# Mixer tiles of a Mamba-2 block: D product moved to the tile's end, x transposed in halves, y's halves added after the masked decays

## The chip, the cores and the metric

One core of a Trainium2 chip runs the whole program. The metric is the device time of one execution in microseconds (us). Of the kernel before there are three timed executions and one more that was profiled. The engines are named as in the profile: PE is TensorE (PEld its weight loads), DVE is VectorE, ACT is ScalarE, POOL is GpSimd, SP is SyncE.

## The reference, cut to what matters

2048 tokens of width 512 (two sequences of 1024) go through an expert feed-forward block, a Mamba-2 mixer and a second feed-forward block. The change touches the mixer alone:

```python
zxbcdt = layernorm(x) @ W_in.T              # z, x, B, C, dt
x, B, C = silu(causal_conv4(xBC) + conv_b)  # x: 16 heads of 64
dt = softplus(dt + dt_bias); dA = exp(-exp(A_log) * dt)
state = dA * state + x[..., None] * (dt * B)     # step by step along the sequence
y = C . state + D * x
yg = y * silu(z)
out = (yg * rsqrt(mean(yg * yg) + eps) * norm_w) @ W_out.T   # added to the residual
```

## The kernel before

The recurrence is worked in tiles of 128 tokens. A sequence is one turn `i` of a loop and has two groups `j` of four tiles `q`, so there are 2 x 2 x 4 = 16 tiles; `n` counts the eight tiles of a turn. Each group begins with nine weight units (projection, convolution, decay sums, the gate z), and then come the four tiles, the subject of the change. In one tile:

- **decays** (PE, `decays(n, q, g)`, L1925 and L1929): for each quarter `g` of the heads the exponent of the masked decay goes into one of two banks; ACT takes the exponential into L (L1006). The next quarter in the same bank waits for that.
- **G** (PE, L1945, L1946): C x B and B transposed; ACT copies both to GB (L1013).
- **x in rows** (PE, L1950): eight transposes into banks 4 and 5. DVE makes xdt = x dt (L1473) and xD = x D (L1485) of them; POOL makes xw from xdt (L722).
- **M**: DVE multiplies L by C x B in place, a quarter at a time (L1497). These instructions read two tiles of SBUF.
- **C x S** (PE, L1966): C times the carried state, into banks 6 and 7; DVE multiplies it by its decays into y, "yc" below (L1508), and POOL adds xD to y (L729).
- **D product** (PE, L1980): B x xw into banks 4 and 5, which DVE adds to the state that POOL has decayed (L717, L1522, L1523).
- **M x xdt** (PE, L1988): 16 matmuls (32 records), one for each head, into banks 6 and 7. DVE adds each half to y (L1529) and POOL multiplies it by silu(z) (L734).
- **The next step for the tile before**: y_features (PE, L1818) transposes the gated y in two halves into banks 6 and 7, ACT writes its high part (`y_hi`) and DVE its low part (`y_lo`, L1057), and project (PE, L1834) multiplies it by W_out. ACT sums the squares (L958), POOL makes the root of their mean (`rms`, L698 to L700), and DVE adds the result to the residual (L1374). For the first tile of a group (q = 0) there is no tile before in its stream: that one's features and projection stand among the next group's first units, or at the end of the turn.
- **The next group's input**: DVE takes statistics of one tile (L1043 to L1049), POOL their root (L614, L615), DVE scales it (L1054), PE transposes it (L1973), ACT and DVE split it (L756, L1057).

The order on each engine is written out by hand and each engine works its own list in order. Semaphores tie the lists: `after(s, n, ...)` waits until `s` has been raised n times in this turn. PE's order in a tile is decays 0 and 1, G, x in rows, decays 2, y_features(n-1), decays 3, project(n-1), C x S, the transposes of the next input, D product, M x xdt. DVE's is statistics, xdt, y_lo(n-1), xD, scale, M 0 to 3, residual(n-1), yc, xb low part, the two state additions, the two additions to y.

Of the kernel before, what the change touches and what calls it, by code (L numbers as in the profile page):

```python
# [8 lines left out]
P = 128  # L9
# [100 lines left out]
def program(nc, x, w_router, w_gate, w_up, w_down, w_in, w_dt, conv, heads, norm_w, w_out, out):  # L110
# [356 lines left out]
    with block:  # L467
# [118 lines left out]
        def _(pool):  # L586
# [84 lines left out]
            def mixer(k):  # L671
# [12 lines left out]
                def turn(i):  # L684
# [17 lines left out]
                    for j in range(BPB):  # L702
# [5 lines left out]
                        for q in range(TB):  # L708
                            n = j * TB + q
                            hq = slice(q * HEADS, (q + 1) * HEADS)  # L710
                            pool.wait_ge(l_var, i * TPB + (n + TB + 1))
                            rsqrt_ln(slice(q, q + 1), l_rstd)
# [6 lines left out]
                                               each(dec[:, hq], HD), ALU.mult).then_inc(m_Sd, 1)  # L719
                            after(m_xdt, n + 1, TPB)  # L720
# [4 lines left out]
                            if q >= 1:  # L725
                                rms(n - 1)
# [23 lines left out]
        def _(act):  # L750
# [157 lines left out]
            def mixer(k):  # L908
# [10 lines left out]
                def turn(i):  # L919
# [40 lines left out]
                    for j in range(BPB):  # L960
# [39 lines left out]
                        for q in range(TB):  # L1000
                            n = j * TB + q
                            for g in range(HG):
                                after(m_B, HG * n + g + 1, HG * TPB)
                                after(m_E, 2 * n, 2 * TPB)
                                for h in range(g * GH, (g + 1) * GH):
                                    ins = act.activation(L[:, h], bank[g % 2][:, (h % GH) * P:(h % GH + 1) * P], ACT.Exp,  # L1006
                                                         bias=ncs[:, q * HEADS + h:q * HEADS + h + 1])
                                ins.then_inc(m_L, 1)
                                if g == 0:
                                    after(m_G, n + 1, TPB)  # L1010
                                    after(m_D, n, TPB)
                                    after(m_M, HG * n, HG * TPB)
                                    act.activation(GB[:], bank[3][:, 0:2 * P], ACT.Copy).then_inc(m_Bt, 1)  # L1013
                                if g == 1 and q >= 1:
                                    y_hi(n - 1)
                            if q >= 1:
                                squares(n - 1)

# [18 lines left out]
        def _(dve):  # L1037
# [314 lines left out]
            def mixer(k):  # L1352
                nf, nm = phase_counts(k)
                wait_residual(dve, k)
                def turn(i):
# [21 lines left out]
                    for j in range(BPB):  # L1377
# [78 lines left out]
                        for q in range(TB):  # L1456
# [8 lines left out]
                            ln_stats([x_next], [q], l_var)  # L1465

                            for half in range(2):
                                hs = slice(half * DI // 2, (half + 1) * DI // 2)
                                after(m_xt, 2 * n + half + 1, 2 * TPB)
                                if half == 0:  # L1470
                                    after(m_xw, n, TPB)
                                    after(m_E, 2 * n, 2 * TPB)
                                ins = dve.tensor_tensor(heads_of(xdt[:, hs]), heads_of(bank[4 + half][:]),  # L1473
                                                        each(dts[:, q * HEADS + half * HB:q * HEADS + (half + 1) * HB], HD),
                                                        ALU.mult)
                                if half == 0:
                                    own.mark(ins)
                            ins.then_inc(m_xdt, 1)
                            if q >= 1:
                                y_lo(n - 1)  # L1480

                            after(m_yd, n, TPB)
                            for half in range(2):
                                hs = slice(half * DI // 2, (half + 1) * DI // 2)
                                ins = dve.tensor_tensor(heads_of(xD[:, hs]), heads_of(bank[4 + half][:]),  # L1485
                                                        each(hp[:, 2 * HEADS + half * HB:2 * HEADS + (half + 1) * HB], HD),
                                                        ALU.mult)
                                if half == 0:
                                    own.mark(ins)
                            ins.then_inc(m_xD, 1)  # L1490
# [4 lines left out]
                            for g in range(HG):  # L1495
                                after(m_L, HG * n + g + 1, HG * TPB)
                                dve.tensor_tensor(L[:, g * GH:(g + 1) * GH], L[:, g * GH:(g + 1) * GH],  # L1497
                                                  some(GB[:, 0:P], GH), ALU.mult).then_inc(m_M, 1)
                            if q >= 1:
                                residual(n - 1)  # L1500

# [4 lines left out]
                            for half in range(2):  # L1506
                                hs = slice(half * DI // 2, (half + 1) * DI // 2)
                                ins = dve.tensor_tensor(heads_of(y[:, n % 2, hs]), heads_of(bank[6 + half][:]),  # L1508
                                                        each(ecs[:, q * HEADS + half * HB:q * HEADS + (half + 1) * HB], HD),
                                                        ALU.mult)  # L1510
                                if half == 0:
                                    own.mark(ins)
                            ins.then_inc(m_yc, 1)
# [3 lines left out]
                                    xb[:, 0, :, q * P:(q + 1) * P], l_lo)  # L1517

# [5 lines left out]

                            after(m_yd, n + 1, TPB)
                            for half in range(2):
# [528 lines left out]
```

## Time and profile before

| what | value |
|---|---|
| median of 3 executions | 1613.78 us (1613.63 to 1614.77) |
| profiled execution, its own time | 1616.87 us |
| its span, first to last instruction | 1615.1 us |
| PE busy | 1522.0 us (94%) |
| DVE busy | 1044.0 us (65%) |
| ACT busy | 750.3 us (46%) |
| POOL busy | 796.0 us (49%) |
| mean granted TensorE clock | 0.976 |

Starts and durations in the trace are counted from the start of the span of 1615.1 us. The profiled execution took 3.1 us more than the median. A granted clock of 1.00 is the engine's 2.4 GHz and 0.50 is 1.2 GHz.

### The profile page before, as it was taken

To read this page: it belongs to the slowest core of one execution; us is meant where nothing else is said; L and a number is where in the kernel's file an instruction comes from. 1 tells how busy PE (TensorE), PEld (TensorE's weight loads), DVE (VectorE), ACT (ScalarE), POOL (GpSimd) and SP (SyncE) were. 2 spreads that over 40 slices of the span, in tenths; PEclk is the share of its full clock that TensorE was granted. 3 is DMA by queue.
4 is the path that set the end of the run, shared out by engine and by line. 5 is a ranking of instruction groups with operands and counts; after the bars stand their busy time and mean duration, and the time that the engine had idled before them with its cause. 6 is when DMAs were issued, how large, how long until landed. Compare 5 with 4: busy or idle time off the path is not lost. (4 is left out here: it accounts for less than half of the span.)

```text
span 1615.1 us, 23935 instructions
## 1 busy us (share of the span) xinstructions
PE 1522.0 (94%) x8530; PEld 1294.3 (80%) x8530; DVE 1044.0 (65%) x1739; ACT 750.3 (46%) x1290; POOL 796.0 (49%) x491
## 2 busy tenths in 40 slices
PE   6989999999999989999988999999889999999999
PEld 6767999989877777787767778778668999999877
DVE  7664565666467877677657767766564666666465
ACT  4211666666512654454445345434222666666411
POOL 2101777776444435535534553553021777666442
PEclk9999999999999999999999999998999999999999
DMA  7032687867443120020012001014222787777243
GB/s 291 27 108 62 215 284 254 283 244 255 173 166 99 53 79 1 17 76 27 1 50 70 1 27 66 1 37 162 69 68 93 249 276 257 270 272 266 75 161 127
DMA packets 70873, 214.42 MB, mean 133 GB/s; under 512 B 8097, under 2 KB 8097, under 8 KB 69857
## 3 DMA queue, kind: packets, MB, share of 16 engines
q1 hardware_dynamic: 48672, 155.18, 27.2%
q0 software_dynamic: 11360, 37.23, 7.8%
q10 hardware_dynamic: 10720, 20.45, 3.5%
q8 instruction: 70, 1.15, 0.3%
q14 instruction: 51, 0.41, 0.1%
HBM read 179.80 MB, written 33.03 MB: 132 GB/s over the span
## 5 line engine op out<-in xcount | busy, mean ns | idle before, releaser
L626 POOL TENSOR_TENSOR g_lo<-g_raw,g_hi 128x1408 fp32r<-128x1408 f32 x54 | 179.4, 3322 | 259.4 <-ACT g_hi L756 258.9
L626 POOL TENSOR_TENSOR u_lo<-u_raw,u_hi 128x1408 fp32r<-128x1408 f32 x54 | 174.5, 3231 | 67.9 <-ACT u_hi L756 67.9
L1674 PE MATMUL bank<-u_hi,xgT 128*128 128x352 f32 x624 | 168.5, 333 | 0.0
L1674 PE MATMUL bank<-g_hi,xgT 128*128 128x352 f32 x624 | 162.7, 323 | 0.0
L1697 PE MATMUL bank<-d_hi,hT 128*128 128x512 f32 (+1 forms) x468 | 159.8, 395 | 1.8 <-DVE hT L1057 1.8
L691 POOL TENSOR_TENSOR w_hl<-w_raw,w_hl 128x1024 fp32r<-128x1024 f32 x36 | 88.8, 2468 | 144.7 <-ACT w_hl L756 144.7
L1626 PE MATMUL bank<-xs,g_hi 128*128 128x512 f32 (+1 forms) x384 | 129.8, 421 | 7.5 <-DVE gate L1203 6.6
L1642 PE MATMUL bank<-d_hi,hT 128*128 128x512 f32 (+1 forms) x384 | 126.1, 401 | 5.9 <-DVE hT L1057 3.5
L804 ACT ACTIVATE gate<-bank 128x512 f32<-128x512 f32 (+1 forms) x48 | 28.6, 596 | 220.5 <-PE bank L1626 212.8
L1057 DVE TENSOR_TENSOR hT<-bank,hT 128x384 fp32r<-128x384 f32 x78 | 43.0, 552 | 128.9 <-ACT hT L756 128.9
L1388 DVE SCALAR_TENSOR_TENSOR acc<-pre,cw,acc 128x512 f32<-128x512 f32 x120 | 121.8, 1015 | 4.3
L1212 DVE TENSOR_TENSOR d_lo<-d_raw,d_hi 128x1024 fp32r<-128x1024 f32 x54 | 106.3, 1968 | 27.2 <-ACT d_hi L756 19.5
L1874 PE MATMUL bank<-xs,w_hl 128*128 128x512 f32 x480 | 115.2, 397 | 7.2 <-issue 5.0
L1626 PE MATMUL bank<-xs,u_hi 128*128 128x512 f32 (+1 forms) x384 | 120.8, 396 | 0.0
L668 POOL DMA_INDIRECT yg<-routed_y,slots x64 | 67.6, 1057 | 97.4 <-DVE X L1235 56.6
L1911 PE MATMUL bank<-w_hl,xs 128*128 128x256 f32 x768 | 101.1, 295 | 14.3 <-ACT zs L989 10.9
L1674 PEld LDWEIGHTS bank<-g_hi,xgT 128*128 128x128 f32 x624 | 111.0, 188 | 3.6
L1874 PEld LDWEIGHTS bank<-xs,w_hl 128*128 128x128 f32 x480 | 90.7, 191 | 28.2 <-issue 8.9
L1911 PEld LDWEIGHTS bank<-w_hl,xs 128*128 128x128 f32 x768 | 98.7, 203 | 16.8 <-ACT zs L989 11.7
L1674 PEld LDWEIGHTS bank<-u_hi,xgT 128*128 128x128 f32 x624 | 110.5, 188 | 0.0
L1057 DVE TENSOR_TENSOR d_lo<-d_raw,d_hi 96x512 fp32r<-96x512 f32 x54 | 109.4, 2025 | 0.0
L1697 PEld LDWEIGHTS bank<-d_hi,hT 128*128 128x128 f32 (+1 forms) x468 | 87.9, 188 | 21.2 <-DVE hT L1057 4.7
(254 smaller groups left out, 3676.8 us busy)
## 6 DMA issues: line engine op xcount, KB each, us to landing
g_raw<-in_w_gate SPq DMA_DIRECT2D x54, 704.0 KB, 5.8
u_raw<-in_w_up SPq DMA_DIRECT2D x54, 704.0 KB, 7.0
d_raw<-in_w_down SPq DMA_DIRECT2D x54, 512.0 KB, 5.3
w_raw<-in_w_in SPq DMA_DIRECT2D x37, 512.0 KB
routed_y<-ys ACTq DMA_DIRECT2D x32, 512.0 KB
d_raw<-in_w_down SPq DMA_DIRECT2D x54, 192.0 KB, 5.6
token_x<-xn SPq DMA_DIRECT2D x8, 1024.0 KB, 5.2
X<-in_x SPq DMA_DIRECT2D x4, 1024.0 KB, 10.1
```

What stands on the lines that cost most here:

```text
L626: pool.tensor_tensor(half_of(piece, 1, s), raw_at[piece][s % RING][:], half_of(piece, 0, s).bitcast(F), ALU.subtract)\
L668: pool.indirect_dma_start(yg[:, t % 2, slot], None, routed_y, slot_rows(slot * NT + t))\
L691: pool.tensor_tensor(w_hl[:, w % 2, 1], w_raw[:, w % 2], w_hl[:, w % 2, 0].bitcast(F), ALU.subtract).then_inc(m_wlo, 1)
L1057: dve.tensor_tensor(hl_lo, value, hl_hi.bitcast(F), ALU.subtract).then_inc(signal, 1)
L1212: dve.tensor_tensor(lo[:, 0:2], raw[:, 0:2], hi[:, 0:2].bitcast(F), ALU.subtract)
L1388: ins = dve.scalar_tensor_tensor(acc[:, c % 2], pre[:, c % 2, tap:tap + D], cw[:, c, tap:tap + 1], acc[:, c % 2], ALU.mult, ALU.add)
L1626: ins = pe.matmul(dst[0:fw, 0:width], half_of(part, hw, s)[:, kc, f0:f0 + fw], x_of(hx, kc), start=(n == 0), stop=(n == 3 * KD - 1))
L1642: ins = pe.matmul(bank[4 + a][:], hT[0:fw, hh, c, a * P:(a + 1) * P], half_of(2, hw, s)[0:fw, c], start=(c == 0 and m == 0), stop=(c == NF ...
L1674: ins = pe.matmul(dst[:, 0:FE], xgT[:, n % 2, hx, kc], half_of(piece, hw, NS + j)[:, kc], start=(m == 0), stop=(m == 3 * KD - 1))
L1697: ins = pe.matmul(bank[Y + n % 2][:], hT[0:fw, hh, c, 0:P], half_of(2, hw, NS + j)[0:fw, c], start=(m == 0), stop=(m == 3 * NF - 1))
L1874: ins = pe.matmul(bank[c % 2][:], wt[:, hw, kc, (c % 2) * P:(c % 2 + 1) * P], xb[:, hx, kc], start=(m == 0), stop=(m == 3 * KD - 1))
L1911: ins = pe.matmul(bank[6 + half][:, (q % 2) * WU:(q % 2 + 1) * WU], xb[:, hx, kc, q * P:(q + 1) * P], wt[:, hw, kc], start=(m == 0), stop= ...
```

## The change

On PE, the two halves of y_features(n-1) stand before decays 0 and after decays 1. The x transposes are split: the first half before G, the second after decays 2. C x S follows; then come decays 3 and project(n-1). M x xdt comes ahead of the D product, which is the last work of the tile. On ACT, `y_hi` of each half stands before the exponentials of quarters 0 and 1; the squares and the copy to GB stand before quarter 2. On DVE, y_lo(n-1) comes first, xdt waits for both halves of x, and then come scale, M 0, xD, yc, M 1 to 3, the low part of xb, the first addition to y, residual(n-1), the second addition to y and the state additions. On POOL, the decay of S comes before the layer-norm root, and rms(n-1) comes before xw. No operation is added or left out. The diff, with the common indentation and blank lines taken off:

```diff
--- before.py
+++ after.py
@@ -708,8 +708,6 @@
 for q in range(TB):
     n = j * TB + q
     hq = slice(q * HEADS, (q + 1) * HEADS)
-    pool.wait_ge(l_var, i * TPB + (n + TB + 1))
-    rsqrt_ln(slice(q, q + 1), l_rstd)
     after(m_dec, j + 1, BPB)
     after(m_C, n, TPB)
     after(m_S, n, TPB)
@@ -717,13 +715,15 @@
     pool.tensor_tensor(S[:, (n + 1) % 2].rearrange("p (h d) -> p h d", d=HD),
                        S[:, n % 2].rearrange("p (h d) -> p h d", d=HD),
                        each(dec[:, hq], HD), ALU.mult).then_inc(m_Sd, 1)
+    pool.wait_ge(l_var, i * TPB + (n + TB + 1))
+    rsqrt_ln(slice(q, q + 1), l_rstd)
+    if q >= 1:
+        rms(n - 1)
     after(m_xdt, n + 1, TPB)
     after(m_D, n, TPB)
     pool.tensor_tensor(xw[:].rearrange("p (h d) -> p h d", d=HD),
                        xdt[:].rearrange("p (h d) -> p h d", d=HD),
                        each(wd[:, hq], HD), ALU.mult).then_inc(m_xw, 1)
-    if q >= 1:
-        rms(n - 1)
     after(m_yc, n + 1, TPB)
     after(m_xD, n + 1, TPB)
     pool.tensor_tensor(y[:, n % 2], y[:, n % 2], xD[:], ALU.add).then_inc(m_yd, 1)
@@ -1000,22 +1000,21 @@
 for q in range(TB):
     n = j * TB + q
     for g in range(HG):
+        if g < 2 and q >= 1:
+            y_hi(n - 1, (g,))
+        if g == 2:
+            if q >= 1:
+                squares(n - 1)
+            after(m_G, n + 1, TPB)
+            after(m_D, n, TPB)
+            after(m_M, HG * n, HG * TPB)
+            act.activation(GB[:], bank[3][:, 0:2 * P], ACT.Copy).then_inc(m_Bt, 1)
         after(m_B, HG * n + g + 1, HG * TPB)
         after(m_E, 2 * n, 2 * TPB)
         for h in range(g * GH, (g + 1) * GH):
             ins = act.activation(L[:, h], bank[g % 2][:, (h % GH) * P:(h % GH + 1) * P], ACT.Exp,
                                  bias=ncs[:, q * HEADS + h:q * HEADS + h + 1])
         ins.then_inc(m_L, 1)
-        if g == 0:
-            after(m_G, n + 1, TPB)
-            after(m_D, n, TPB)
-            after(m_M, HG * n, HG * TPB)
-            act.activation(GB[:], bank[3][:, 0:2 * P], ACT.Copy).then_inc(m_Bt, 1)
-        if g == 1 and q >= 1:
-            y_hi(n - 1)
-    if q >= 1:
-        squares(n - 1)
     act.wait_ge(l_tp, i * TPB + (n + TB + 1))
     split_hi(xb[:, 0, :, q * P:(q + 1) * P], bank[3][:].rearrange("p (c t) -> p c t", c=KD), l_hi)
 y_hi(TPB - 1)
@@ -1462,72 +1461,69 @@
         nxt = dve.snap(nxt % NT)
     x_next = X[:, bass.ds(nxt, 1), :].rearrange("p o n -> p (o n)")
-    ln_stats([x_next], [q], l_var)
-    for half in range(2):
+    def halves(tile, coefs, width, signal):
+        for half in range(2):
+            hs = slice(half * DI // 2, (half + 1) * DI // 2)
+            ins = dve.tensor_tensor(heads_of(tile[:, hs]), heads_of(bank[width + half][:]),
+                                    each(coefs[half], HD), ALU.mult)
+            if half == 0:
+                own.mark(ins)
+        ins.then_inc(signal, 1)
+    of_heads = lambda t, at: [t[:, at + half * HB:at + (half + 1) * HB] for half in range(2)]
+    def decayed(g):
+        after(m_L, HG * n + g + 1, HG * TPB)
+        dve.tensor_tensor(L[:, g * GH:(g + 1) * GH], L[:, g * GH:(g + 1) * GH],
+                          some(GB[:, 0:P], GH), ALU.mult).then_inc(m_M, 1)
+    def y_add(half):
         hs = slice(half * DI // 2, (half + 1) * DI // 2)
-        after(m_xt, 2 * n + half + 1, 2 * TPB)
-        if half == 0:
-            after(m_xw, n, TPB)
-            after(m_E, 2 * n, 2 * TPB)
-        ins = dve.tensor_tensor(heads_of(xdt[:, hs]), heads_of(bank[4 + half][:]),
-                                each(dts[:, q * HEADS + half * HB:q * HEADS + (half + 1) * HB], HD),
-                                ALU.mult)
-        if half == 0:
-            own.mark(ins)
-    ins.then_inc(m_xdt, 1)
+        after(m_E, 2 * n + half + 1, 2 * TPB)
+        dve.tensor_tensor(y[:, n % 2, hs], y[:, n % 2, hs], bank[6 + half][:], ALU.add)\
+            .then_inc(m_yi, 1)
     if q >= 1:
         y_lo(n - 1)
-    after(m_yd, n, TPB)
-    for half in range(2):
-        hs = slice(half * DI // 2, (half + 1) * DI // 2)
-        ins = dve.tensor_tensor(heads_of(xD[:, hs]), heads_of(bank[4 + half][:]),
-                                each(hp[:, 2 * HEADS + half * HB:2 * HEADS + (half + 1) * HB], HD),
-                                ALU.mult)
-        if half == 0:
-            own.mark(ins)
-    ins.then_inc(m_xD, 1)
+    ln_stats([x_next], [q], l_var)
+    after(m_xt, 2 * n + 2, 2 * TPB)
+    after(m_xw, n, TPB)
+    after(m_E, 2 * n, 2 * TPB)
+    halves(xdt, of_heads(dts, q * HEADS), 4, m_xdt)
     dve.wait_ge(l_rstd, i * TPB + (n + TB + 1))
     dve.wait_ge(l_tp, i * TPB + (n + TB - 1))
     ln_scale(xn_m[:, q % 2], x_next, q).then_inc(l_xn, 1)
     after(m_Bt, n + 1, TPB)
-    for g in range(HG):
-        after(m_L, HG * n + g + 1, HG * TPB)
-        dve.tensor_tensor(L[:, g * GH:(g + 1) * GH], L[:, g * GH:(g + 1) * GH],
-                          some(GB[:, 0:P], GH), ALU.mult).then_inc(m_M, 1)
-    if q >= 1:
-        residual(n - 1)
+    decayed(0)
+    after(m_yd, n, TPB)
+    halves(xD, of_heads(hp, 2 * HEADS), 4, m_xD)
     after(m_C, n + 1, TPB)
     after(m_dec, j + 1, BPB)
     after(m_F, 2 * (n - 1), 2 * TPB)
     after(m_sq, n - 1, TPB)
-    for half in range(2):
-        hs = slice(half * DI // 2, (half + 1) * DI // 2)
-        ins = dve.tensor_tensor(heads_of(y[:, n % 2, hs]), heads_of(bank[6 + half][:]),
-                                each(ecs[:, q * HEADS + half * HB:q * HEADS + (half + 1) * HB], HD),
-                                ALU.mult)
-        if half == 0:
-            own.mark(ins)
-    ins.then_inc(m_yc, 1)
+    halves(y[:, n % 2], of_heads(ecs, q * HEADS), 6, m_yc)
+    decayed(1)
+    decayed(2)
+    decayed(3)
     dve.wait_ge(l_hi, i * TPB + (n + TB + 1))
     lo_half(xb[:, 1, :, q * P:(q + 1) * P], bank[3][:].rearrange("p (c t) -> p c t", c=KD),
             xb[:, 0, :, q * P:(q + 1) * P], l_lo)
+    after(m_yd, n + 1, TPB)
+    y_add(0)
+    if q >= 1:
+        residual(n - 1)
+    y_add(1)
     after(m_D, n + 1, TPB)
     after(m_Sd, n + 1, TPB)
     new = S[:, (n + 1) % 2]
     own.mark(dve.tensor_tensor(new[:, 0:DI // 2], new[:, 0:DI // 2], bank[4][:], ALU.add))
     dve.tensor_tensor(new[:, DI // 2:DI], new[:, DI // 2:DI], bank[5][:], ALU.add).then_inc(m_S, 1)
-    after(m_yd, n + 1, TPB)
-    for half in range(2):
-        hs = slice(half * DI // 2, (half + 1) * DI // 2)
-        after(m_E, 2 * n + half + 1, 2 * TPB)
-        dve.tensor_tensor(y[:, n % 2, hs], y[:, n % 2, hs], bank[6 + half][:], ALU.add)\
-            .then_inc(m_yi, 1)
 y_lo(TPB - 1)
 residual(TPB - 1)
 settle((m_xw, TPB), (m_yd, TPB), (m_E, 2 * TPB), (m_F, 2 * TPB), (m_sq, TPB), (m_out, TPB),
@@ -1934,28 +1930,31 @@
 for q in range(TB):
     n = j * TB + q
     tt = slice(q * P, (q + 1) * P)
+    def x_rows(half):
+        for c in range(4):
+            ins = pe.transpose(bank[4 + half][:, c * P:(c + 1) * P],
+                               xc[:, 2 + 4 * half + c, tt], ident[:])
+        ins.then_inc(m_xt, 1)
+    if q >= 1:
+        y_features(n - 1, (0,))
     decays(n, q, 0)
     decays(n, q, 1)
+    if q >= 1:
+        y_features(n - 1, (1,))
     if q == 0:
         after(m_xc, (j + 1) * NCH, BPB * NCH)
+    after(m_S, n, TPB)
+    x_rows(0)
     after(m_Bt, n, TPB)
     after(m_dtc, j + 1, BPB)
     pe.wait_ge(l_lo, i * TPB + (n + TB))
     pe.matmul(bank[3][:, 0:P], xc[:, 0, tt], xc[:, 1, tt], start=True, stop=True)
     pe.transpose(bank[3][:, P:2 * P], xc[:, 0, tt], ident[:]).then_inc(m_G, 1)
-    after(m_S, n, TPB)
-    for half in range(2):
-        for c in range(4):
-            ins = pe.transpose(bank[4 + half][:, c * P:(c + 1) * P],
-                               xc[:, 2 + 4 * half + c, tt], ident[:])
-        ins.then_inc(m_xt, 1)
     decays(n, q, 2)
-    if q >= 1:
-        y_features(n - 1)
-    decays(n, q, 3)
-    if q >= 1:
-        project(n - 1)
+    x_rows(1)
     pe.wait_ge(m_zero, i + 1)
     after(m_yi, 2 * n, 2 * TPB)
@@ -1966,6 +1965,9 @@
         ins = pe.matmul(bank[6 + half][:], xc[:, 1, tt], S[:, n % 2, half * 512:(half + 1) * 512],
                         start=True, stop=True)
     ins.then_inc(m_C, 1)
+    decays(n, q, 3)
+    if q >= 1:
+        project(n - 1)
     pe.wait_ge(l_xn, i * TPB + (n + TB + 1))
     after(m_Bt, n + 1, TPB)
@@ -1974,14 +1976,7 @@
                            ident[:])
     ins.then_inc(l_tp, 1)
-    after(m_xw, n + 1, TPB)
-    after(m_xD, n + 1, TPB)
-    for half in range(2):
-        ins = pe.matmul(bank[4 + half][:], Bt, xw[:, half * 512:(half + 1) * 512],
-                        start=True, stop=True)
-    ins.then_inc(m_D, 1)
     after(m_yc, n + 1, TPB)
     for g in range(HG):
         after(m_M, HG * n + g + 1, HG * TPB)
         for h in range(g * GH, (g + 1) * GH):
@@ -1989,6 +1984,13 @@
                             xdt[:, h * HD:(h + 1) * HD], start=True, stop=True)
         if g % 2:
             ins.then_inc(m_E, 1)
+    after(m_xw, n + 1, TPB)
+    after(m_xD, n + 1, TPB)
+    for half in range(2):
+        ins = pe.matmul(bank[4 + half][:], Bt, xw[:, half * 512:(half + 1) * 512],
+                        start=True, stop=True)
+    ins.then_inc(m_D, 1)
 y_features(TPB - 1)
 project(TPB - 1)
```

## Rows read from the trace of the kernel before

**Rows 1.** Waits of PE, 537 to 1092 us: who waited for whom, us in total, times, longest.
```profile
PE bank L1834 <- DVE yT L1057: 7.5, 12, 0.6
```
**Rows 2.** Timeline, a later tile (q = 2): start us, us, engine, line, operation, count.
```profile
633.12 0.38 PE L1925 MATMUL bank<-mask_b,ident_b 128*128 128x512 bf16 x1
...
635.70 1.04 PE L1818 MATMUL bank<-ident,y 128*128 128x128 f32 x8
...
636.34 1.09 ACT L756 ACTIVATE yT<-bank 128x512 fp32r<-128x512 f32 x2
...
636.97 1.29 DVE L1057 TENSOR_TENSOR yT<-bank,yT 128x512 fp32r<-128x512 f32 x2 [0.56 <-ACT yT L756]
...
637.81 5.69 PE L1834 MATMUL bank<-wo,yT 128*128 128x512 f32 x24 [0.63 <-DVE yT L1057]
...
643.33 1.88 PE L1966 MATMUL bank<-S,xc 128*128 128x512 f32 x4
...
645.49 1.88 PE L1980 MATMUL bank<-xw,GB 128*128 128x512 f32 x4
...
647.20 3.68 PE L1988 MATMUL bank<-xdt,L 128*128 128x64 f32 x32
...
649.21 0.69 DVE L1529 TENSOR_TENSOR y<-y,bank 128x512 f32<-128x512 f32 x1 [0.52 <-PE bank L1988]
649.97 1.27 POOL L734 TENSOR_TENSOR y<-y,zs 128x512 f32<-128x512 f32 x1 [1.00 <-DVE y L1529]
...
650.72 0.38 PE L1925 MATMUL bank<-mask_b,ident_b 128*128 128x512 bf16 x1
```
**Rows 3.** Timeline, the same tile: what DVE and POOL do.
```profile
633.92 0.69 DVE L1043 BATCH_NORM_STATS2 stats<-X 128x6 f32 x1
...
635.12 1.29 DVE L1473 TENSOR_TENSOR xdt<-bank,dts 128x512 f32<-128x512 f32 x2
...
638.18 1.28 DVE L1485 TENSOR_TENSOR xD<-bank,hp 128x512 f32<-128x512 f32 x2
...
640.07 2.49 DVE L1497 TENSOR_TENSOR L<-L,GB 128x512 f32<-128x512 f32 x4
...
646.62 2.36 POOL L729 TENSOR_TENSOR y<-y,xD 128x1024 f32<-128x1024 f32 x1 [4.26 <-DVE y L1508]
```
**Rows 4.** Timeline, a group's first tile (q = 0).
```profile
600.93 0.39 PE L1925 MATMUL bank<-mask_b,ident_b 128*128 128x512 bf16 x1
...
602.85 1.29 DVE L1473 TENSOR_TENSOR xdt<-bank,dts 128x512 f32<-128x512 f32 x2 [1.76 <-PE bank L1950]
...
603.40 1.15 ACT L1006 ACTIVATE L<-bank,ncs 128x128 f32<-128x128 f32 x4
...
604.60 0.39 PE L1925 MATMUL bank<-mask_b,ident_b 128*128 128x512 bf16 x1 [1.36 <-ACT L L1006]
...
605.53 2.08 POOL L722 TENSOR_TENSOR xw<-xdt,wd 128x1024 f32<-128x1024 f32 x1
605.78 2.38 DVE L1497 TENSOR_TENSOR L<-L,GB 128x512 f32<-128x512 f32 x1
...
606.36 3.63 PE L1966 MATMUL bank<-S,xc 128*128 128x512 f32 x4
...
611.99 3.68 PE L1988 MATMUL bank<-xdt,L 128*128 128x64 f32 x32
```
**Rows 5.** Windows, the same tile: us, busy of PE, PEld, DVE, ACT, POOL, clock, DMA.
```profile
607.00:608.00 1.00, 1.00 (x2) 0.34 (x1) 1.00 (x1) 0.92 (x4) 0.61 (x1) 0.50 0.00 0
```
**Rows 6.** Timeline, a group's units: the convolution's three taps, undisturbed, then with POOL.
```profile
679.26 2.33 DVE L1388 SCALAR_TENSOR_TENSOR acc<-pre,cw,acc 128x512 f32<-128x512 f32 x3
...
681.70 4.35 DVE L1388 SCALAR_TENSOR_TENSOR acc<-pre,cw,acc 128x512 f32<-128x512 f32 x3
...
681.97 2.75 POOL L691 TENSOR_TENSOR w_hl<-w_raw,w_hl 128x1024 fp32r<-128x1024 f32 x1
```
**Rows 7.** Timeline, PE at the end of the first turn.
```profile
798.48 3.68 PE L1988 MATMUL bank<-xdt,L 128*128 128x64 f32 x32
...
804.99 7.04 PE L1834 MATMUL bank<-wo,yT 128*128 128x512 f32 x24
```

## The prediction

> **What bounds the kernel now.** I read the page first, for the shares: PE is busy nearly throughout, so time is won only where PE waits. Then I read PE's waits over the mixer. The one wait that each later tile (q = 1 to 3) repeats is the projection's for the low part of the transposed y: 12 times, 7.5 us in all [rows 1]. The timeline of one such tile shows why: transposes at 635.70, ACT's high part at 636.34, DVE's low part at 636.97, projection at 637.81, after a wait of 0.63. The tile lasts 650.72 - 633.12 = 17.60 us [rows 2]. From rows of PE I take strides (start to start): projection 643.33 - 637.81 = 5.52, M x xdt with the step to the next tile 3.52 (3.42 without), D product 647.20 - 645.49 = 1.71 and C x S the same; eight transposes 0.88, a quarter's decays 0.44, G 0.38, the input's four transposes 0.44 [rows 2].
>
> The first tile of a group is another matter: there the time goes by DVE. From 600.93 on, xdt starts after 1.92 us. The first masked decay then takes 2.38 us, where four take 2.49 in a later tile [rows 3, 4]. It stood at 605.78 and ended 0.55 after POOL's xw ended at 607.61: while POOL works, a DVE instruction that reads two tiles of SBUF stands still. After three more of about 0.6, the decays end at 609.97, as does C x S at 609.99, though that ran at clock 0.50 (1.2 GHz) [rows 4, 5]: the low clock cost next to nothing there. M x xdt starts at 611.99, 11.06 us into the tile. With 3.52 the tile is 14.58.
>
> **The change, later tiles.** Let s be the start of the first half of y_features.
> - The previous M x xdt began at s - 5.2 (3.42, D product 1.71, a step of 0.07). DVE adds y's first half 2.01 after its start and POOL's gating ends 4.04 after it [rows 2], so the first transposes don't wait. The second half's gating ends near 5.75, s + 0.55, and its transposes come at s + 1.32.
> - ACT follows by 0.64: y_hi 0 at s + 0.64, exponentials (1.15) from s + 1.13, y_hi 1 at s + 2.2. DVE's low part follows by 0.63, at s + 2.83, and PE by 0.84 after that: C x S at s + 3.67. PE's own work ahead of it is 3 x 0.44 of decays, 0.88 of y, 0.88 of x and 0.38 of G, 3.46. What is left of the wait is 0.2, now before C x S.
> - Then C x S 1.71, decays 0.44, projection 5.52 and transposes 0.44: M x xdt at s + 11.78, the next tile at s + 17.0. I take **0.6 gained** on each of 12 tiles, 7.2 us. Both ends: nothing gained, or 0.8 with no wait at all.
> - The cover on DVE: low part to s + 3.5, statistics 1.2, xdt 1.25, scale 0.7 at most (between xD's end and M [rows 3]), M 0 0.6, xD and yc 2.5: yc ends at s + 9.7. M 1 to 10.3; POOL's addition of xD (2.36) goes next and holds M 2 back until 12.7, ended at 13.3, M 3 at 13.9. PE needs M 2 at 11.78 + 1.71 = 13.5 and M 3 at 14.35. It holds, by 0.2 us. With this cover gone, each microsecond of delay is one of the tile.
> - xw is behind rms on POOL, and so behind M 0 on DVE, by some 0.4 us. The D product needs xw only at s + 15.2. POOL's root of the statistics is now behind the decay of S, done by s + 3.4, before the statistics exist. No DMA is moved, and SP has no part in a tile.
>
> **The first tiles.** Here nothing hides the new order. Quarter 2's decays wait for ACT's first exponentials: 603.40 + 1.15, PE at 604.60, which is 3.67 [rows 4]. Half of x now stands behind them, at 4.11. DVE's xdt needs both halves and starts 0.64 later, at 4.75 instead of 1.92, and ends at 6.04. POOL's xw begins at 6.1 and goes ahead of M 0, as before, since scale stands between xdt and M 0: xw ends at 8.2, M 0 at 8.8. xD and yc (2.4) end at 11.2. M x xdt starts at 11.35, only 0.3 later than before. But M 1 to 3 are now behind yc: M 1 ends at 11.8, POOL adds xD until 14.05, M 2 ends at 14.6, M 3 at 15.2. PE does two quarters by 13.1, waits, starts quarter 2 at 14.75, has both by 16.5, and then the D product: 18.2 instead of 14.58, **3.6 lost**.
>
> That POOL gets in between M 1 and M 2 is the disputed price. The nearest row: taps at 681.70 took 4.35 instead of 2.33, and POOL's instruction 2.75 [rows 6], so POOL waited for one tap and then held up the other two. Those taps are parted by waits, M 1 to 3 are not. If POOL comes last instead, y waits for it and the next tile starts at about 17.4: 2.8 lost. I take the first value, as the row is of the same two engines.
>
> The Trainium skill ("SBUF — State Buffer", Who interferes with whom) says that VectorE with two SBUF inputs and a GpSimd instruction that reads SBUF exclude each other, and "Issue order, not op shape, decides who blocks". It speaks against this change, which puts M 1 to 3 right beside POOL's addition, where before they stood ahead of it. The trace agrees, with the 2.38 of the first M [rows 4]. By the page alone M 1, issued first, holds POOL, and then POOL holds M 2, which is the same 3.6.
>
> **The clock** fell to 0.50 in such a tile before [rows 5], after PE had waited for ACT, and for about 3.5 us, as C x S took 3.63 instead of 1.88 [rows 2, 4]. In the new order PE waits about 2.4 us before M x xdt and 1.65 between quarters. A second fall would now meet work on the path: 3.5 us at half speed add up to 1.7. I take 0.3, since much of it would fall into waits. So a first tile costs 3.9, bounded by 1.2 (the faster rival, below) and 3.6 + 1.7 = 5.3; four cost **15.6**.
>
> **End of a turn** (two). Before, from M x xdt to the projection 804.99 - 798.48 = 6.51 [rows 7], with the D product 1.71 ahead: 8.22. Now 5.2, then transposes with a wait of 0.15, ACT 0.64 after their start, the low part behind the state additions at 6.6, projection at 7.4. Gained 0.8 each, **1.7**. The 24 matmuls took 7.04 there instead of 5.69; if the clock stays up, 1.35 more each. Groups that end without a turn gain nothing of their own.
>
> **Sum**: 15.6 - 7.2 - 1.7 = +6.7. The profiled execution, at 1616.87, would go to 1623.6. It stands 3.1 above the median, so the median goes to 1613.78 + 6.7, about **1620**, 0.4% slower. About 0.2% (3.2 us) is what a measurement of this kernel can tell from no change.
>
> **The rivals.**
> - *Forecast (0.58)*: later tiles gain, first tiles lose more. With its bounds 1616 (2.8 lost in each first tile: 11.2 - 8.9 = +2.3) to 1631 (5.3 lost, and 0.2 gained in a later tile: 21.2 - 2.4 - 1.7 = +17.1).
> - *Faster (0.18)*: VectorE isn't held up in the first tiles. If M 0 goes ahead of xw, yc ends at 9.5; if M 1 to 3 go ahead of POOL's addition, M x xdt runs through from 9.65 and y's chain ends the tile near 15.8. Lost 1.2: 4.8 - 7.2 - 1.7 = -4.1, 1609.7. For it: in later tiles rms's small instructions did not slow the four M. Against: the 2.38. It decides when a first tile loses less than 1.4 us.
> - *About the same (0.18)*: only one of the two goes VectorE's way, 2.3 lost: 9.2 - 8.9 = +0.3, 1614. A weaker form: gain and loss are each a third off.
> - *Much slower (0.06)*: in later tiles xw starts ahead of M 0 and takes 1.9 us off a cover of 0.2. A tile becomes 1.2 longer than before: 15.6 + 14.4 - 1.7 = +28, 1642. Against it: rms stands before xw.
>
> **Range.** 1610 to 1631 takes in the forecast with its bounds and the same-time case, and the edge of the faster one; it leaves out most of the faster and the much slower case. Faster 0.18, same 0.20, slower 0.62.
>
> **What would show it.** Later tiles: period near 17.0, no wait before the projection, 0.2 before C x S. First tiles: xdt about 4.75 after the first decays, an M of over 2 us beside xw and another beside POOL's addition, PE waiting for M between quarters 1 and 2 of M x xdt, tile near 18.2. Turn end: projection 0.8 earlier. The prediction is wrong if first tiles stay under 16 us, or later ones stay at 17.6.

## The result, and the profile of the kernel after

The median went from 1613.7 us (1612.38 to 1614.77, four runs) to **1635.88 us** (1633.47 to 1637.94, four runs): a ratio of 1.0137, with a 95% interval of [1.0117, 1.0157]. Slower was the likeliest sign of the prediction. Its 1620 is 16 us too low, though, and the time lies outside its range of 1610 to 1631. The profiled execution took 1637.94 us with a span of 1636.2, so the spans differ by 21.1.

The page first. PE is busy for 12.7 us more (1522.0 before) with the same 8530 instructions, and four more slices show a clock under 0.9: its matmuls have become slower. DVE is busy for 27.9 us more (1044.0 before) with the same 1739 instructions: its masked decays, which now stand still beside POOL, take 82.8 us instead of 46.6, and its other instructions 8.3 less.

```profile
span 1636.2 us, 23919 instructions
...
PE 1534.7 (94%) x8530; PEld 1302.9 (80%) x8530; DVE 1071.9 (66%) x1739; ACT 749.4 (46%) x1290; POOL 798.7 (49%) x491
...
PEclk9999999999999998998999899898999999999999
```

The waits of PE over the mixer (537 to 1112 us) of the kernel after, answering to [rows 1]; the columns are the total in us, the number and the longest:

```profile
PE bank L1983 <- DVE y L1468: 14.5, 4, 4.0
...
PE bank L1921 <- ACT L L1015: 7.4, 4, 1.8
...
PE bank L1830 <- DVE yT L1056: 2.1, 2, 1.1
...
PE bank L1983 <- DVE L L1479: 1.3, 2, 0.8
```

The projection's twelve waits (7.5 us) are gone; the two that are left are the turn ends. In their place stand four waits of M x xdt for yc, one in each group's first tile, 14.5 us in all. The wait for M 2, on which the prediction spent most of its words, is 1.3 us in two tiles.

A later tile (q = 1 of the first group) of the kernel after, rows of PE, DVE and POOL from its timeline, answering to [rows 2, 3]; the columns are start and duration in us, engine, line, operation and count:

```profile
624.86 0.60 PE L1814 MATMUL bank<-ident,y 128*128 128x128 f32 x4
...
627.65 0.69 DVE L1056 TENSOR_TENSOR yT<-bank,yT 128x512 fp32r<-128x512 f32 x1 [0.70 <-ACT yT L756]
...
628.49 1.96 PE L1965 MATMUL bank<-S,xc 128*128 128x512 f32 x4
...
631.11 0.69 DVE L1479 TENSOR_TENSOR L<-L,GB 128x512 f32<-128x512 f32 x1
...
631.57 1.99 POOL L724 TENSOR_TENSOR xw<-xdt,wd 128x1024 f32<-128x1024 f32 x1
...
634.10 4.08 DVE L1479 TENSOR_TENSOR L<-L,GB 128x512 f32<-128x512 f32 x3
...
636.71 3.68 PE L1983 MATMUL bank<-xdt,L 128*128 128x64 f32 x32
...
642.00 0.60 PE L1814 MATMUL bank<-ident,y 128*128 128x128 f32 x4
```

With s = 624.86 the low part comes at s + 2.79, C x S at s + 3.63, M x xdt at s + 11.85 and the next tile at s + 17.14. The prediction had 2.83, 3.67, 11.78 and 17.0. The addition of xD does get between the three M (4.08 instead of 1.9), but PE never waits for them.

The first tile of the second group of the kernel after, answering to [rows 4]:

```profile
742.51 0.39 PE L1921 MATMUL bank<-mask_b,ident_b 128*128 128x512 bf16 x1
...
747.27 1.29 DVE L1468 TENSOR_TENSOR xdt<-bank,dts 128x512 f32<-128x512 f32 x2 [4.58 <-PE bank L1936]
...
748.64 2.13 POOL L724 TENSOR_TENSOR xw<-xdt,wd 128x1024 f32<-128x1024 f32 x1 [0.78 <-DVE xdt L1468]
...
748.93 2.39 DVE L1479 TENSOR_TENSOR L<-L,GB 128x512 f32<-128x512 f32 x1
...
753.64 4.04 DVE L1479 TENSOR_TENSOR L<-L,GB 128x512 f32<-128x512 f32 x3
753.77 7.04 PE L1983 MATMUL bank<-xdt,L 128*128 128x64 f32 x32 [3.93 <-DVE y L1468]
753.80 2.73 POOL L729 TENSOR_TENSOR y<-y,xD 128x1024 f32<-128x1024 f32 x1 [3.02 <-DVE y L1468]
...
760.61 3.73 PE L1991 MATMUL bank<-xw,GB 128*128 128x512 f32 x4
...
764.12 0.73 PE L1814 MATMUL bank<-ident,y 128*128 128x128 f32 x4
```

And the granted clock there, from the windows of the same kernel (stretch; clock in the third column from the right). A window's mean tells how much of it was at 0.50: 0.57 means 0.86 us of it, 0.81 means 0.38.

```profile
753.00:754.00 1.00, 0.23 (x2) 0.23 (x3) 1.00 (x3) 0.00 (x0) 0.20 (x1) 1.00 0.00 0
754.00:755.00 1.00, 1.00 (x7) 1.00 (x7) 1.00 (x2) 0.00 (x0) 1.00 (x1) 0.57 0.00 0
...
758.00:759.00 1.00, 1.00 (x7) 1.00 (x6) 0.88 (x2) 0.00 (x0) 0.04 (x1) 0.50 0.00 0
764.00:765.00 1.00, 1.00 (x8) 0.74 (x7) 0.63 (x2) 0.11 (x1) 0.00 (x0) 0.81 0.00 0
```

Up to M x xdt the tile goes as worked out: xdt at 4.76, M x xdt at 11.26. Then the clock falls to 0.50 (1.2 GHz) at 754.14, 0.37 us into M x xdt and right behind PE's wait of 3.93, and comes back at 764.38, 10.2 us later, after the D product. M x xdt took 7.04 instead of 3.68, the D product 3.73 instead of 1.94. The same 10.2 us stand in all four first tiles (in the first group the fall comes inside the wait, at 614.19), where the kernel before had one stretch of 3.4 under C x S [rows 5]. Up to the next tile's transposes a tile lasts 21.6 to 21.7 us. In the last two groups the low clock reaches into the next tile; counted from the first decays to the next M x xdt, less the 11.85 of an undisturbed tile, the four are 21.7 to 22.1, 21.9 in the mean, against 14.57 before.

**The books.** Four first tiles: 4 x 7.3 = 29.2 lost. Twelve later ones, at 17.11 to 17.14 instead of 17.60: 6.0 gained. Two turn ends: 4.1 gained (below). Together +19.1 of the 21.1. The rest stands ahead of the first group, whose first decays come at 603.19 instead of 600.93, 2.3 later; the trace after has one low-clock stretch more there (563 to 566). The change does not touch that part; in the profiled executions of the twelve experiments the same decays come anywhere from 596.87 (9) to 602.68 (11), so it is spread between executions.

### The profile page after: what moved, and what is told of

The parts are those of the page before. It is cut to its first block and busy times, and to the rows that moved or that the text cites. A ratio compares the mean times of both kernels' runs of the same rounds, so it can differ in the third digit from the quotient of the medians.

```text
span 1636.2 us, 23919 instructions
## 1 busy us (share of the span) xinstructions
PE 1534.7 (94%) x8530; PEld 1302.9 (80%) x8530; DVE 1071.9 (66%) x1739; ACT 749.4 (46%) x1290; POOL 798.7 (49%) x491
## 3 DMA queue, kind: packets, MB, share of 16 engines
q8 instruction: 70, 1.15, 0.3%
## 5 line engine op out<-in xcount | busy, mean ns | idle before, releaser
L1907 PEld LDWEIGHTS bank<-w_hl,xs 128*128 128x128 f32 x768 | 98.5, 203 | 16.3 <-ACT zs L989 11.7
```

What stands on the lines that cost most here:

```text
L1907: ins = pe.matmul(bank[6 + half][:, (q % 2) * WU:(q % 2 + 1) * WU], xb[:, hx, kc, q * P:(q + 1) * P], wt[:, hw, kc], start=(m == 0), stop= ...
```

## The experiments

Three things had to be told apart: whether the first tiles alone lose, what in them costs the clock, and what the POOL additions beside the masked decays cost. The first four kernels were made from the two shown, with the order chosen by q. Each group's first tile is q == 0. "To M x xdt" is from the first decays of a first tile to its M x xdt; "on" is from there to the next tile's M x xdt. Before: 11.0 and 17.6; after: 11.3 to 11.7, and 21.85 to 22.7. Each ratio is to executions of the kernel before that were timed alongside (medians 1613.53 to 1614.25), so it need not be the quotient of two medians given here.

**1. The new order in the later tiles alone.** On PE, ACT, DVE and POOL:

```diff
+if q >= 1:
     (order of after)
+else:
+    (order of before)
```

> The first tile of a group (q = 0) is in the old order on all engines, the later tiles in the new one. If gain and loss sit where the two traces put them, a first tile is 14.6 us again, a later one stays 17.1, and the turn ends stay as after the change: 1613.7 - 12 x 0.5 - 2 x 2.2 = about 1603 to 1606, faster than both kernels. Rival (the new order of the later tiles only pays because the first tile has shifted the engines against each other): later tiles go back to 17.6 and the time to about 1613.

1607.65 us (1605.91 to 1612.99, ten runs), ratio 0.9958 [0.9944, 0.9972]. This half of the change is a gain. It falls 2 us short of 1606. The first tile lasts 15.1 us instead of 14.6, as it ends with M x xdt and the next one now begins with the transposes of its y: PE waits for the gated y eight times, 2.3 us in all.

**2. The new order in the first tile alone**, the same edit with `q == 0`.

> Only the first tile of a group is in the new order, the later ones in the old. If the loss is all in the first tiles: 21.6 us each instead of 14.6, 4 x 7.0 = 28 more, later tiles 17.6, about 1641. Rival (the clock stays low because of what the later tiles do behind it): first tiles near 18.2 and the time near 1628.

1641.43 us, ratio 1.0185 [1.0168, 1.0202]. The clock is at 0.50 for 10.2 to 13.7 us in each first tile, which lasts about 22. The two halves of the change add up: 1607.65 + 1641.43 - 1613.7 = 1635.4, and both together measured 1635.88.

**3. Matmuls that keep the clock up.** Outputs that nobody reads, into a free bank: ten ahead of M x xdt, in what is PE's wait, and seven between its quarters 1 and 2. This filler is extra work for PE alone.

```diff
+if q == 0: filler(10)      # bf16, 512 columns, result unused
 after(m_yc, n + 1, TPB)
 for g in range(HG):
+    if q == 0 and g == 2: filler(7)
```

> The changed kernel, and in each first tile PE multiplies something nobody reads while it waits: 10 bf16 matmuls of 512 columns ahead of M x xdt and 7 between its quarters 1 and 2 (2.1 and 1.5 us at full clock, less than the waits). Theory (the clock's fall is what the prediction priced too low): the clock stays at 1.00, M x xdt takes 3.4 us plus the wait for M 2, a first tile 18.2 us as predicted, and the time is 1636 - 4 x 3.4 = about 1622. Rival (VectorE's late M 2 and M 3 set the tile's end, the low clock only fills the wait): a first tile stays above 21 us and the time at 1636.

1625.66 us (1621.43 to 1632.29, four runs), ratio 1.0093 [1.0067, 1.0118]: by the medians 10 us less than the kernel after, by added work, and no execution of the one reaches into those of the other (1633.47 to 1637.94). By the ratios it is 7 us. The profiled execution, the fastest of the four, has clock 1.00 through all four M x xdt. Its second group's first tile, from the timeline:

```profile
747.83 4.03 DVE L1504 TENSOR_TENSOR L<-L,GB 128x512 f32<-128x512 f32 x3
...
747.96 2.00 PE L2100 MATMUL bank<-xdt,L 128*128 128x64 f32 x16 [1.89 <-DVE y L1493]
749.80 1.68 PE L2040 MATMUL bank<-mask_b,ident_b 128*128 128x512 bf16 x7
...
751.32 2.00 PE L2100 MATMUL bank<-xdt,L 128*128 128x64 f32 x16
...
753.15 1.94 PE L2034 MATMUL bank<-xw,GB 128*128 128x512 f32 x4
```

Two quarters in 2.00; the next two start 3.36 after them instead of 1.71, so 1.65 later for the M that POOL delays (4.03), the value predicted; D product 1.94: this is the tile that the prediction worked out. From 736.51 to the next tile's start at 754.92 it lasts 18.41; predicted were 18.2.

**4. POOL's addition behind all four M** of a first tile.

```diff
 after(m_xD, n + 1, TPB)
+if q == 0: after(m_M, HG * (n + 1), HG * TPB)
 pool.tensor_tensor(y, y, xD, ALU.add)
```

> The changed kernel, and in each first tile POOL adds xD to y only when all four M are done, so VectorE is not held up between M 1 and M 2. Theory (at the low clock two quarters of M x xdt take 3.4 us, as long as M 2 is held up): M 3 is ready some 2.3 us sooner and the tile stays at 21.6, the time at 1634 to 1636. Rival (the port): M x xdt finds its quarters ready and the tile goes below 19.5, the time below 1628.

1631.96 us (1628.7 to 1635.45, four runs), ratio 1.0125 [1.0107, 1.0143]. This lies between the 1634 of the theory and the 1628 of the rival, and isn't clear of the kernel after, whose interval it overlaps. The trace speaks for the theory: the clock is low for 10.2 us in each first tile as before, and counted as above the tiles are 21.6 to 21.8, 0.2 shorter in the mean. At half clock, two quarters take about as long as M 2 is held up, so the collision is hidden behind the slow matmuls. Where the other 3 us between the medians come from is open; the first decays of this profiled execution come 4.5 us sooner.

**5. Both**: ten fillers ahead and POOL last (no filler between the quarters).

> The changed kernel with both cures in each first tile: 10 matmuls nobody reads ahead of M x xdt, and POOL adds xD to y only after all four M. Theory (at full clock the held-up M 2 is the bound, as the prediction said, and POOL's late addition the next one): M x xdt and the D product run through, y's chain ends the tile near 17.5 us, one less than with the filler alone (18.6 in its trace): 4 us faster than that kernel. Rival (the port never sets the end): no change against the filler alone.

1625.59 us, ratio 1.0085 [1.006, 1.011], no better than experiment 3, a miss. The profile is mixed: in two first tiles "on" is 18.17 and 18.20, 0.6 less than in 3, so the collision is worth this much once the clock is up. In the other two the clock fell (614.5 to 621.3, 897.8 to 904.6) and "on" is 20.5.

**6 to 8. One move at a time, on top of kernel 1**, whose first tile has the old order. The D product behind M x xdt, with the state additions behind y's:

```diff
 if q == 0:
-    d_product()
     for g in range(HG): m_x_xdt(g)
+    d_product()
```

> As e1_later_only, but in each first tile the D product stands behind M x xdt (and the state additions behind those to y); the rest of that tile is in the old order. By the working of the prediction: M x xdt starts 0.4 us sooner, at 10.6, and the D product, which filled a wait before, is added: tile 15.8 instead of 14.6, 5 us over e1_later_only, about 1613. Rival (this is the move that lets the clock fall, as PE has nothing to do before M x xdt): the clock is at 0.50 through M x xdt, the tile is 19 us or more and the time over 1624.

1617.26 us (1612.72 to 1623.87, ten runs), ratio 1.0023 [1.0005, 1.004]. That is between theory and rival, and so is the profile. In the one first tile whose clock was up from M x xdt on, "on" is 17.24, as worked out. In the other three it fell for 6.8 to 10.2 us, and "on" is 20.5 to 22.2. This move alone is enough to bring the low clock onto M x xdt in some tiles; PE's wait ahead of M x xdt was 2.49, 0.73 and 0.81 in those three and 0.94 in the one.

The second half of x behind decays 2 (`x_rows(1)` behind `decays(n, q, 2)`):

> As e1_later_only, but in each first tile the second half of x is transposed behind quarter 2's decays; the rest of that tile is in the old order. Theory (the late x costs little by itself, since VectorE had 2.4 us of being held up by xw in that place): M x xdt starts at 11.1 to 11.5, the D product still fills PE's wait, tile 14.6 to 15.0, time 1608 to 1610. Rival (the late x is what the first tile loses by): M x xdt starts 2 us later or more, 1616 or above.

1613.36 us (1609.47 to 1618.62, ten runs), ratio 1.0005 [0.9992, 1.0019]. This is neither the 1608 to 1610 of the theory nor the 1616 of the rival. The profiled execution shows M x xdt 0.3 later (0.7 in the first group) and "on" 0.2 longer in each first tile, 2.3 us over kernel 1's in the end, but the medians are 5.7 apart. What the unprofiled runs did more is open.

M 1 to 3 behind yc (`decayed(0); yc; decayed(1..3)`):

> As e1_later_only, but in each first tile M 1 to 3 stand behind yc on VectorE; the rest of that tile is in the old order. Theory (POOL's addition of xD gets in between M 1 and M 2): M 2 is held up by over 2 us, PE waits for it between quarters 1 and 2, the tile is 15.6 to 16, time about 1613. If the clock falls in that wait as well, 1620 or more. Rival (back to back the M keep POOL out): no wait of PE, tile 14.6, 1608.

1624.41 us (1621.79 to 1625.15, four runs), ratio 1.007 [1.0047, 1.0092]. The second group's first tile:

```profile
743.65 4.04 DVE L1507 TENSOR_TENSOR L<-L,GB 128x512 f32<-128x512 f32 x3
...
743.81 2.72 POOL L746 TENSOR_TENSOR y<-y,xD 128x1024 f32<-128x1024 f32 x1 [2.16 <-DVE y L1496]
...
744.40 1.89 PE L2111 MATMUL bank<-xdt,L 128*128 128x64 f32 x16
...
747.14 2.00 PE L2111 MATMUL bank<-xdt,L 128*128 128x64 f32 x16 [0.85 <-DVE L L1507]
...
751.48 1.11 PE L1894 MATMUL bank<-ident,y 128*128 128x128 f32 x4 [2.34 <-POOL y L751]
```

Here the collision is seen by itself: three M in 4.04, PE waits 0.85 for M 2 and then 2.34 for the gated y. The clock falls inside the second wait and is low for 6.8 us (749.94 to 756.77), into the next tile.

**9 and 10. Where must the filler stand?** Three behind each quarter of M x xdt, none ahead (9); twelve between quarters 1 and 2, none ahead (10). Both on the kernel after.

```diff
 for g in range(HG):
+    if q == 0 and g == 2: filler(12)       # 10
     m_x_xdt(g)
+    if q == 0: filler(3)                   # 9
```

> The changed kernel, with three bf16 matmuls of 512 columns that nobody reads behind each quarter of M x xdt in the first tiles, and none ahead of it, so that the clock falls before M x xdt as it does now. PE has no waits between the quarters now; the question is why the clock stays at 0.50 for some 10 us. Theory (M x xdt itself, 64 columns to each weight load, does not bring it back): with columns between its quarters the clock is back after about 3.4 us, as under C x S in the kernel before, and in spite of 12 more matmuls a first tile is about 21 us. Rival (once fallen it stays for 10 us whatever PE does): low for 10 us, the tile 24 us, the time 2.4 x 4 = 10 us over the changed kernel.

1642.19 us (two runs), ratio 1.0175 [1.015, 1.02], and 10.2 to 13.7 us at 0.50: the theory that fillers between the quarters bring the clock back fell. They add to the time instead: in the trace the tiles last 24.1 to 25.9 us.

> The changed kernel, with nothing ahead of M x xdt and twelve bf16 matmuls of 512 columns that nobody reads between its quarters 1 and 2 in the first tiles (5.1 us at half clock). Theory (a stretch of nothing but 512-column matmuls brings the clock back as under C x S, M x xdt does not): the clock falls as M x xdt starts and is back 3.4 to 7 us later, within or right behind the twelve, and quarters 2 and 3 and the D product run at full clock. Rival (once fallen at that place it stays for 10 us whatever PE does): the low stretch is 10 us again.

1640.06 us (two runs), ratio 1.0158 [1.0129, 1.0188]. Twelve in a row do bring it back before quarter 2, in all four tiles. In three it was low for 6.8 us. In the first group's for 10.2, but there it fell earlier, at 609.77, inside PE's wait, and was back at 620.01, again within the twelve. The second group's tile, timeline, then the first group's twelve and what follows them, then windows of the second group:

```profile
752.87 3.47 PE L2122 MATMUL bank<-xdt,L 128*128 128x64 f32 x16 [4.04 <-DVE y L1501]
756.13 4.65 PE L2053 MATMUL bank<-mask_b,ident_b 128*128 128x512 bf16 x12
760.62 1.90 PE L2122 MATMUL bank<-xdt,L 128*128 128x64 f32 x16
```

```profile
615.25 5.11 PE L2053 MATMUL bank<-mask_b,ident_b 128*128 128x512 bf16 x12
620.20 1.90 PE L2122 MATMUL bank<-xdt,L 128*128 128x64 f32 x16
```

```profile
756.50:757.50 1.00, 1.00 (x4) 0.39 (x3) 1.00 (x3) 0.00 (x0) 0.00 (x0) 0.50 0.00 0
...
760.25:761.25 1.00, 1.00 (x10) 0.85 (x8) 0.00 (x0) 0.00 (x0) 0.00 (x0) 1.00 0.00 0
```

Sixteen matmuls before the twelve take 3.47, sixteen behind them 1.90, and the D product 1.94 in all four tiles. But by then the filler has cost more than it saves: the tiles last 22.6 to 23.3 us.

**11 and 12. A first tile made from what was learned.** Kernel 1 with the D product last, xw on POOL behind all four M (so that none is held up), and fillers in three of PE's waits: four ahead of decays 2, three ahead of decays 3, five ahead of M x xdt. Kernel 12 is the same without the fillers.

```diff
 if q == 0:
+    filler(4); decays(n, q, 2)
+    filler(3); decays(n, q, 3)
     ...
+    filler(5)
     for g in range(HG): m_x_xdt(g)
+    d_product()
 # POOL
+if q == 0: after(m_M, HG * (n + 1), HG * TPB)
 pool.tensor_tensor(xw, xdt, wd, ALU.mult)
```

> Later tiles new, first tile in the old order with three moves: POOL makes xw only after the four M (so it does not hold VectorE up), the D product stands behind M x xdt, and PE fills its waits with matmuls nobody reads (4 before quarter 2's decays, 3 before quarter 3's, 5 before M x xdt). Theory: C x S and all after it runs at full clock, M ends at 7.3 and yc at 8.7, M x xdt starts near 8.9 instead of 11.05, and with the D product behind it the tile is 14.1 us instead of 15.1: 4 us under e1_later_only, about 1603.5. Rival (the clock falls in spite of the filler, or POOL's later xw delays the D product): 1608 or above.

> As g2_first_tile_mended without the matmuls that nobody reads: what they are worth. Theory: C x S runs at 0.50 as in the kernel before, yc ends at 10.4, PE waits 1.3 us before M x xdt at 10.5, and in most executions the clock falls again, as with the D product last: first tiles 16 us or 19 to 20 us, time 1613 to 1622. Rival (the filler does nothing): equal to g2_first_tile_mended.

With fillers **1602.18 us** (1599.66 to 1605.66, six runs), ratio 0.9923 [0.9909, 0.9937], faster than both kernels. Without them 1611.91 (1606.5 to 1618.28, twelve runs), ratio 0.998 [0.9965, 0.9996]. Twelve unused matmuls in each of four tiles are worth 10 us. The first group of the one with fillers:

```profile
602.68 0.39 PE L2006 MATMUL bank<-mask_b,ident_b 128*128 128x512 bf16 x1
...
607.53 1.88 DVE L1512 TENSOR_TENSOR L<-L,GB 128x512 f32<-128x512 f32 x3
...
610.33 1.24 PE L2053 MATMUL bank<-mask_b,ident_b 128*128 128x512 bf16 x5
...
611.66 3.79 PE L2122 MATMUL bank<-xdt,L 128*128 128x64 f32 x32
...
615.28 1.94 PE L2047 MATMUL bank<-xw,GB 128*128 128x512 f32 x4
...
617.05 0.60 PE L1899 MATMUL bank<-ident,y 128*128 128x128 f32 x4
```

and the same two steps without fillers:

```profile
607.58 4.82 PE L2122 MATMUL bank<-xdt,L 128*128 128x64 f32 x32 [1.17 <-DVE y L1501]
...
612.20 3.73 PE L2047 MATMUL bank<-xw,GB 128*128 128x512 f32 x4
```

With fillers the clock is 1.00 in all four first tiles, the three M take 1.88, M x xdt starts 8.98 after the first decays and the tile lasts 14.37. Without, PE waits 1.36, 0.69 and 1.17 in the first group's tile, the last of them ahead of M x xdt, and in three of the four tiles the clock fell for 6.8 us onto M x xdt or the D product. In the fourth it fell only under C x S, and M x xdt took 3.79.

## Why the prediction was right in its sign and short in its size

- **Later tiles: right.** 17.14 against 17.0, M 0 ahead of xw (631.11 against 631.57), the cover on DVE held. 6.0 gained for 7.2 predicted. The first experiment shows this half by itself as a gain.
- **First tiles up to M x xdt: right.** xdt at 4.76 (4.75), M x xdt at 11.26 (11.35), M 0 in 2.39, M 1 to 3 in 4.04 with POOL's addition at 2.73. The faster rival, VectorE not held up, is out, and so is the one of about the same time, as both M 0 and M 2 were held up. The Trainium skill ("SBUF — State Buffer", Who interferes with whom) has a VectorE instruction with two SBUF inputs and a GpSimd instruction that reads SBUF exclude each other; the trace agrees, with 2.39 instead of about 0.6 for the first M. It agrees with "issue order" too: POOL's addition was issued 0.16 after M 1 and took 2.73 instead of 2.36 [rows 3], so it stood behind M 1; it ended at 756.53 and the three M 1.15 later, which is two of them, so M 2 stood behind it. The 18.2 of the whole tile is what experiment 3 shows as 18.4 once the clock is kept up.
- **The clock term: wrong, and this is the step that failed.** "3.5 us at half speed add up to 1.7. I take 0.3, since much of it would fall into waits." It had three faults. The low clock did not last 3.5 us but 10.2, three times what [rows 5] and C x S showed. It did not fall into waits: the wait (3.93, where I had 2.4, since C x S now ran at the full clock, 1.88, in three of the four tiles) came first and the fall at its end or just behind it, so it lay on M x xdt and the D product, which are the path to the tile's end. And its upper bound of 1.7 was made from the length of one earlier stretch. From the strides, M x xdt to the D product took 6.84 instead of 5.07, the D product to the next tile 3.51 instead of 1.8: 3.5 a tile for 0.3. Four times the difference, 13, is most of the 16 us by which the prediction missed. With the clock kept up, experiment 3 measured 1625.66, inside the range.
- **What the fall hid.** The 1.65 between quarters 1 and 2 was worked out for the full clock; at half clock it was 0.5 and 0.8 in two tiles and next to nothing in two. The mechanism (POOL between M 1 and M 2) is real, but here it costs about 0.2 a tile in the trace of experiment 4, and 0.6 a tile with the clock up (experiment 5).

**Turn ends: right, a little short.** M x xdt to the projection, from the timeline of the kernel after:

```profile
810.30 3.68 PE L1983 MATMUL bank<-xdt,L 128*128 128x64 f32 x32
...
817.82 5.68 PE L1830 MATMUL bank<-wo,yT 128*128 128x512 f32 x24 [1.06 <-DVE yT L1056]
```

7.52 + 5.68 = 13.20, against 1.71 + 6.51 + 7.04 = 15.26 of [rows 7] with the D product ahead: 2.06 gained, and 2.0 at the second turn end. The prediction had 0.8, "if the clock stays up, 1.35 more each". It stayed up.

**The rivals.** "Much slower" forecast 1642, near what came, but by xw ahead of M 0 in later tiles, and there M 0 was ahead. The number was near for another reason.

What stays open: why the low clock lasts through M x xdt, although PE's row is full in its windows; how short a wait is enough to bring the fall, as waits of 0.6 to 1.2 us were followed by it in some tiles and not in others; and why the executions of the kernels with partial fillers spread so far (1621 to 1632 in experiment 3). Only one execution of each was profiled.

## What to carry to other kernels

An order that makes PE wait in front of a long run of small matmuls can cost more than the wait: price that run at half clock up to its end, not by the length of a low stretch seen elsewhere. Here it did so in every tile with a wait of 2.65 to 3.96 us, and in three tiles of four with waits of 0.6 to 1.2 us (experiment 12). Test it by putting matmuls whose results nobody reads into the wait; they are free there, and were worth 10 us here (1602.2 against 1611.9), while the same matmuls behind the fall cost time. And where a loop's first pass has nothing to overlap with, give it an order of its own: the change helped in twelve tiles (0.9958) and hurt in four (1.0185).

## What the runs showed of the hardware

- **A low clock can outlast a full PE row.** Under 512-column fp32 matmuls (C x S in the kernel before) the clock was back after 3.4 us. When it fell ahead of the 32 matmuls of 64 columns, each with its own 128x128 weights, it stayed at 0.50 through the rest of them, although the window 758:759 has PE at 1.00, and came back only in or behind the D product, 2.7 to 4.6 us after those four 512-column matmuls had begun: 10.2 us in all, up to 13.7 in experiments 2 and 9.
- **Three bf16 matmuls behind each eight small ones did not bring it back sooner; twelve in a row did.** With three it was low for 10.2 to 13.7 us; with twelve it was back in all four tiles, 3.3 to 4.8 us after the first of them (experiments 9 and 10).
- **POOL gets in between two VectorE instructions that follow each other at once.** Three M took 4.03 to 4.09 in every tile in which POOL's addition (2.72 to 2.77) was issued beside them, 1.88 where it was held behind them (experiments 4 and 5).
- **The same order gave both levels within one execution**: without fillers, one first tile of four kept the full clock through M x xdt (experiments 6 and 12). A single tile, or a single profile, doesn't settle such a question.
